# Three engines' share of a layer norm moved to one: GpSimd takes all but VectorE's statistics

## The chip, the cores and the metric

The kernel runs on one core of a Trainium2 chip, as one launch. The metric is the device time of that launch in microseconds. Engines are called by the profile's names: PE is TensorE (PEld its weight loads), DVE is VectorE, ACT is ScalarE, POOL is GpSimd, SP is SyncE. They run side by side, each through its own list of instructions in a fixed order, and wait for each other on semaphores.

## The reference

The input is x, 8 sequences of 256 tokens with 128 features, all float32. Four blocks follow each other, each of the form x + f(layernorm(x)):

- a state-space block (Mamba style) with 16 states: its own RMS norm, a projection, a 4-tap convolution, softplus steps, a scan over time per state, a gate, an output projection;
- a mixture of 8 experts with 352 inner features, top 2 of 8 (called FFN here);
- an attention block with squared ReLU scores;
- the same mixture of experts again.

What matters here is the norm in front of each block:

```python
def _layernorm(x, axis=-1, eps=1e-05):
    m = jnp.mean(x, axis=axis, keepdims=True)
    v = jnp.var(x, axis=axis, keepdims=True)
    return (x - m) / jnp.sqrt(v + eps)
```

In front of the state-space block an RMS norm with its own epsilon follows. Both are folded into one factor per token: (variance times (1 + 1e-6) + 1e-11) to the power -1/2.

So there are 4 norms for each of 8 sequences: 8 called `m_*` (state-space) and 24 called `n_*` (16 in front of an FFN, 8 in front of attention).

## The kernel before

Tokens lie on the 128 partitions, so that a sequence is two halves (c = 0 and 1) of 128 tokens by 128 features: `X[:, u, c, :]`. A norm makes two tiles 128x128 (`m_xn` or `n_xn`), PE transposes them into a PSUM bank, ACT rounds them to a high part (`xhi`), DVE takes the remainder (`xlo`), and from then on PE multiplies with three products per weight tile (lines 1028 to 1030).

Who does what in a norm before the change:

- DVE, `m_stats`/`n_stats`: `bn_stats` for each half (line 798), `bn_aggr` for each half (line 801), then variance plus epsilon on a 128x2 tile (`m_ve` line 811, `n_ve` line 916).
- POOL, `m_pow`/`n_pow`: that tile to the power -1/2 (lines 407 and 414), giving `m_r`/`n_r`.
- DVE, `m_nb`/`n_nb`: minus mean times that factor (lines 816 and 921), giving `m_b`/`n_b`.
- ACT, `m_norm`/`n_norm`: factor times x plus that bias, one instruction for each half (lines 533 and 652), with one signal behind the second.
- PE, `m_turn`/`n_turn`: two transposes (line 1023) behind that one signal.

The order of all the work is set by one plan. `build_plan` gives every step of every sequence a due time from hand-set tables (`AT`, `NORM`, `M_IN`, `SHIFT`, ...), sorts the steps by it, and each engine issues its own steps in that order (`run_schedule`). The state-space scan of sequence u overlaps the FFNs and attention of the sequences before it, one period of some 70 us for each sequence; behind the last scan only FFN and attention work is left.

POOL's steps in the scan of one sequence are, for each of 16 states, a product with C (`mulC`, line 455, waits for DVE's scan of that state, line 891) and a running sum (`sum`, line 468), about 1.3 us each; then the convolution (lines 426 and 437), `m_delta` (line 447) and `m_gate` (line 475). The due time of `n_norm` lies 1.5 us behind that of `n_pow`. In the sorted plan a step of POOL's scan work falls between the two for almost every `n` norm of a sequence whose scan is still running, for example:

```
n_pow(q3), sum(3,0), n_norm(q3), m_norm(4), mulC(3,1)
n_pow(q8), mulC(5,9), n_norm(q8), sum(5,9)
```

Here q counts the 16 FFNs in their order, so that q0 is the first FFN of sequence 0, and odd q (up to 13) are first FFNs, even q from 2 on second FFNs; a0 to a7 are the attention norms; (3,1) is state 1 of sequence 3. For q0 a `mulC(1,0)` stands between `n_pow` and `n_norm`, and for the attention norm a3 the first product of a convolution (`m_mul1(6)`). Behind the last scan nothing stands between them.

Of the kernel before, what the change touches and what calls it, by code (L numbers as in the profile page):

```python
# [5 lines left out]
ALU = mybir.AluOpType  # L6
# [47 lines left out]
 m_var m_rstd m_nb m_xm m_xt m_hi m_lo m_ph m_pad m_tap0 m_tap m_sum m_conv0 m_h m_xp m_xe m_dt m_abs m_e m_u m_ln m_v m_pos m_delta m_dx m_y0  # L54
 m_pg m_g m_dA m_dbx m_scan m_p m_ysum m_yacc m_yg m_out m_x1
 n_var n_rstd n_nb n_xm n_xt n_hi n_lo r_lg r_dd r_th r_w2 r_w
# [11 lines left out]
M_IN = {"m_stats": -0.78, "m_pow": -1.32, "m_nb": -0.06, "m_norm": 1.88, "m_turn": 2.37, "m_hi": 3.09, "m_lo": 2.98,  # L68
# [5 lines left out]
NORM = {"n_stats": -0.39, "n_pow": 1.17, "n_nb": 1.18, "n_norm": 2.67, "n_turn": 3.85, "n_hi": 4.96, "n_lo": 4.64}  # L74
# [14 lines left out]
SHIFT = {"m_stats": [0.5, -67.8, -1.1], "m_pow": [-15.2, -60.3, -0.2], "m_nb": [0.2, -65.6, 0],  # L89
         "m_norm": [-11.5, -58.6, 0.2], "m_turn": [0.1, -59.4, 2.5], "m_hi": [0.3, -54.7, 0.5],  # L90
# [95 lines left out]
def build(nc, x, vecs, in_w, xproj_w, dt_w, out_w, gate_w, up_w, down_w, uv_w, wo_w, row_b, router_w, out):  # L186
    schedule = build_plan()
    norms = norm_order(schedule)
    with ExitStack() as ctx:
# [46 lines left out]
        m_b = sb("m_b", [P, NC])  # L236
# [23 lines left out]
        n_b = sb("n_b", [P, NC])  # L260
# [131 lines left out]
        def _(pool):  # L392
# [84 lines left out]
            run_schedule({"setup": setup, "m_pow": m_pow, "n_pow": n_pow, "m_mul1": conv_product(1), "m_add1": conv_sum(1),  # L477
# [4 lines left out]
        def _(act):  # L482
# [43 lines left out]

            def m_norm(u):

                act.wait_ge(s["m_nb"], u + 1)
                if u:  # L530
                    act.wait_ge(s["m_xt"], u)
                for c in range(NC):
                    ins = nc.scalar.activation(m_xn[:, c, :], X[:, u, c, :], ACT.Identity, bias=m_b[:, c:c + 1],
                                               scale=m_r[:, c:c + 1])
                ins.then_inc(s["m_xm"], 1)
# [108 lines left out]
            def n_norm(arg):  # L644
                l = norms[arg]
                kind, k = arg
# [663 lines left out]
```

## Time and profile before

| what | value |
|---|---|
| median of 3 runs | 674.01 us (668.97 to 675.3) |
| profiled execution, its own time | 673.67 us |
| its span, first to last instruction | 672.1 us |
| PE busy | 583.7 us (87%) |
| DVE busy | 527.1 us (78%) |
| POOL busy | 400.0 us (60%) |
| ACT busy | 395.5 us (59%) |
| mean granted TensorE clock | 0.937 |

The profiled execution's time is its span and 1.57 us around it, and lies 0.34 us under the median. Busy shares are means over stages with different limits: up to about 62 us the first scan runs with little else, from 62 to 566 us scans, FFNs and attention overlap, and from 566 us on POOL has only the norms' powers to do.

### The profile page before, as it was taken

Reading aid. Unit: us, or ns where it says so; the run is one execution under the profiler, and the core shown is the slowest. Engines: PE = TensorE matmul, PEld = TensorE weight load, DVE = VectorE, ACT = ScalarE, POOL = GpSimd, SP = SyncE. Lnnn points to the kernel's source line nnn. Section 1 sums busy time; section 2 is a strip of 40 time slices with the busy share of each in tenths; the row PEclk is TensorE's granted clock in tenths of the full one; section 3 lists DMA queues with packets and bytes.
Section 4 is the critical chain, followed back from the end, with each engine's and each line's share of the span. In section 5 each row is a group of like instructions: output and inputs, shape, how many; then the busy total and the mean of one; then the engine's idle time right before and its main releaser. Section 6 shows DMA issues by size and latency. Waiting matters only on the chain.

```text
span 672.1 us, 12742 instructions
## 1 busy us (share of the span) xinstructions
PE 583.7 (87%) x4370; PEld 550.3 (82%) x4370; DVE 527.1 (78%) x1162; ACT 395.5 (59%) x804; POOL 400.0 (60%) x338
## 2 busy tenths in 40 slices
PE   2566891399896999999999989999999999999998
PEld 1222791299896998989998989899989999999998
DVE  5789898667788789997899879988998897545454
ACT  6877566256567584777567674967585741515230
POOL 1296699858566586849775976778775665000000
PEclk9978896579798798989999998999997999999999
DMA  8725013111111110121122112031204000000000
GB/s 297 266 74 189 13 67 125 63 32 54 59 72 63 72 60 31 63 82 65 68 73 77 71 65 76 11 136 66 75 2 145 1 13 1 22 1 13 1 21 9
DMA packets 18162, 45.30 MB, mean 67 GB/s; under 512 B 2799, under 2 KB 13488, under 8 KB 13746
## 3 DMA queue, kind: packets, MB, share of 16 engines
q1 hardware_dynamic: 18098, 44.49, 18.9%
q8 instruction: 35, 0.57, 0.4%
q14 instruction: 29, 0.24, 0.1%
HBM read 40.02 MB, written 1.31 MB: 61 GB/s over the span
## 4 chain that ended last, share of the span: by engine, by line
PE 65%; DVE 11%; POOL 7%; issue 5%; ACT 3%; DVEq 0%; ACTq 0%; POOLq 0%
PE ps L1179 15%; PE ps L1028 14%; PE ps L1030 14%; PE ps L1029 14%; POOL yacc L468 3%; POOL st L455 2%; DVE X L992 2%; PE ps L1228 2%; DVE st L891 2%; DVE ps L877 1%; PE ps L1096 1%; PE ps L1241 1%; PE ps L1219 1%; DVE n_bn L798 1%; ACT L489 1%
## 5 line engine op out<-in xcount | busy, mean ns | idle before, releaser
L455 POOL TENSOR_TENSOR st<-st,rows_ring 128x512 f32<-128x512 f32 x128 | 168.1, 1314 | 98.1 <-DVE st L891 97.9
L1179 PE MATMUL ps<-down,inner_ring 128*128 128x128 f32 (+1 forms) x1408 | 172.2, 275 | 0.0
L1179 PEld LDWEIGHTS ps<-down,inner_ring 128*128 128x128 f32 (+1 forms) x1408 | 166.3, 192 | 1.1 <-DVE X L992 0.2
L686 ACT ACTIVATE sg<-ps 128x512 f32<-128x512 f32 x176 | 104.9, 597 | 100.9 <-PE ps L1030 99.0
L891 DVE TENSOR_TENSOR_SCAN st<-dA,ps 128x512 f32<-128x512 f32 x128 | 155.4, 1214 | 5.6 <-PE ps L1129 2.5
L978 DVE TENSOR_TENSOR inner_ring<-sg,ps 128x512 f32<-128x512 f32 x176 | 119.1, 679 | 47.5 <-ACT sg L686 24.7
L468 POOL TENSOR_TENSOR yacc<-yacc,st 128x512 f32<-128x512 f32 x112 | 144.5, 1290 | 7.1
L1028 PE MATMUL ps<-xhi,gate_hi 128*128 128x256 f32 x352 | 105.8, 301 | 19.0 <-DVE xlo L928 19.0
L641 ACT ACTIVATE dA<-delta,A 128x255 f32<-128x255 f32 x256 | 105.8, 494 | 8.5 <-POOL delta L447 7.4
L1028 PE MATMUL ps<-xhi,up_hi 128*128 128x256 f32 x352 | 106.3, 302 | 0.4 <-DVE inner_ring L978 0.3
L1029 PE MATMUL ps<-xlo,up_hi 128*128 128x256 f32 x352 | 102.9, 292 | 0.0
L1030 PE MATMUL ps<-xhi,up_lo 128*128 128x256 f32 x352 | 102.8, 292 | 0.0
L1029 PE MATMUL ps<-xlo,gate_hi 128*128 128x256 f32 x352 | 102.6, 291 | 0.0
L1030 PE MATMUL ps<-xhi,gate_lo 128*128 128x256 f32 x352 | 102.5, 291 | 0.0
L877 DVE TENSOR_TENSOR ps<-ps,rows_ring 128x512 f32<-128x512 f32 x128 | 88.4, 691 | 1.2
L1028 PEld LDWEIGHTS ps<-xhi,gate_hi 128*128 128x128 f32 x352 | 70.5, 200 | 22.6 <-issue 14.1
L992 DVE SCALAR_TENSOR_TENSOR X<-ps,wts,X 128x128 f32<-128x128 f32 x256 | 76.0, 342 | 13.7 <-PE ps L1179 13.7
L1028 PEld LDWEIGHTS ps<-xhi,up_hi 128*128 128x128 f32 x352 | 70.8, 201 | 1.4 <-DVE inner_ring L978 1.2
L1029 PEld LDWEIGHTS ps<-xlo,up_hi 128*128 128x128 f32 x352 | 71.0, 202 | 0.1
L1030 PEld LDWEIGHTS ps<-xhi,up_lo 128*128 128x128 f32 x352 | 70.8, 201 | 0.0
L1029 PEld LDWEIGHTS ps<-xlo,gate_hi 128*128 128x128 f32 x352 | 70.6, 201 | 0.1
L1030 PEld LDWEIGHTS ps<-xhi,gate_lo 128*128 128x128 f32 x352 | 70.5, 200 | 0.0
(145 smaller groups left out, 812.3 us busy)
## 6 DMA issues: line engine op xcount, KB each, us to landing
rows_ring<-bc SPq DMA_DIRECT2D x32, 1024.0 KB, 4.8
moved_rows<-inner_ring SPq DMA_DIRECT2D x96, 32.0 KB, 1.8
inner_ring<-gate_w SPq DMA_DIRECT2D x1, 1408.0 KB, 8.3
inner_ring<-up_w SPq DMA_DIRECT2D x1, 1408.0 KB, 10.8
down<-down_w SPq DMA_DIRECT2D x2, 512.0 KB, 10.8
out<-X SPq DMA_DIRECT2D x8, 128.0 KB, 1.8
X<-x SPq DMA_DIRECT2D x1, 896.0 KB, 5.4
down<-down_w SPq DMA_DIRECT2D x1, 384.0 KB, 8.4
```

The costliest lines, as they stand in the source:

```text
L455: nc.gpsimd.tensor_tensor(st[:, i % NST], st[:, i % NST], row, ALU.mult).then_inc(s["m_p"], 1)
L468: nc.gpsimd.tensor_tensor(yacc[:, u % 2], yacc[:, u % 2], st[:, i % NST], ALU.add).then_inc(s["m_yacc"], 1)
L641: ins = nc.scalar.activation(dA[:, i % NDA, it, 1:], delta[:, it, 1:], ACT.Exp, scale=A[:, it, n:n + 1])
L686: nc.scalar.activation(sg[:, k % 2], two(bank_of(q, 2 * j)), ACT.Silu).then_inc(s["f_sg"], 1)
L877: nc.vector.tensor_tensor(states_in(u, n), dxps, row, ALU.mult).then_inc(s["m_dbx"], 1)
L891: nc.vector.tensor_tensor_scan(out=st[:, i % NST].rearrange(flat), data0=dA[:, i % NDA].rearrange(flat), data1=states_in(u, n).rearrange(f ...
L978: nc.vector.tensor_tensor(inner[:, j], sg[:, k % 2], two(bank_of(q, 2 * j + 1)), ALU.mult).then_inc(s["f_in"], 1)
L992: nc.vector.scalar_tensor_tensor(out=X[:, u, c, :], in0=part, scalar=wts[:, q % 2, c, e:e + 1], in1=X[:, u, c, :], op0=ALU.mult, op1=ALU.a ...
L1028: nc.tensor.matmul(bank, w[0], xv[0], start=start, stop=False)
L1029: nc.tensor.matmul(bank, w[0], xv[1], start=False, stop=False)
L1030: return nc.tensor.matmul(bank, w[1], xv[0], start=False, stop=stop)
L1179: ins = nc.tensor.matmul(bank_of(q, 2 * NP + e)[:, c * H:(c + 1) * H], act_in, down[0:rows, e, n, :], start=n == 0, stop=n == NB - 1)
```

## The change

DVE keeps the statistics and signals each `bn_aggr`. POOL does the rest: variance plus epsilon, power, and (x - mean) times factor for each half, each half with its own signal. PE waits for the signal of a half in front of the transpose of that half. The DVE steps `m_nb` and `n_nb` are gone, and the steps `m_norm` and `n_norm` keep their due times but are now in POOL's list and not in ACT's. DVE's `n_stats` (and `m_stats` from the second on) newly waits until POOL has done the norm before it, since POOL now reads the mean from `n_mv`.

```diff
@@ POOL
             def m_pow(u):
-                pool.wait_ge(s["m_var"], u + 1)
+                pool.wait_ge(s["m_var"], NC * (u + 1))
+                nc.gpsimd.tensor_scalar(m_ve[:], m_mv[:, :, 1], 1.0 + RMS_EPS, RMS_EPS * EPS, ALU.mult,
+                                        ALU.add).then_inc(s["m_eps"], 1)
+                pool.wait_ge(s["m_eps"], u + 1)
                 nc.gpsimd.tensor_tensor(m_r[:], m_ve[:], neghalf[:], ALU.pow).then_inc(s["m_rstd"], 1)
 
+            def m_norm(u):
+                pool.wait_ge(s["m_rstd"], u + 1)
+                if u:
+                    pool.wait_ge(s["m_xt"], u)
+                for c in range(NC):
+                    nc.gpsimd.tensor_scalar(m_xn[:, c, :], X[:, u, c, :], m_mv[:, c, 0:1], m_r[:, c:c + 1], ALU.subtract,
+                                            ALU.mult).then_inc(s["m_xm"], 1)
+
             def n_pow(arg):
+                pool.wait_ge(s["n_var"], NC * (norms[arg] + 1))
+                nc.gpsimd.tensor_scalar(n_ve[:], n_mv[:, :, 1], EPS, None, ALU.add).then_inc(s["n_eps"], 1)
+                pool.wait_ge(s["n_eps"], norms[arg] + 1)
+                nc.gpsimd.tensor_tensor(n_r[:], n_ve[:], neghalf[:], ALU.pow).then_inc(s["n_rstd"], 1)
+
+            def n_norm(arg):
                 l = norms[arg]
-                pool.wait_ge(s["n_var"], l + 1)
+                kind, k = arg
+                u = k if kind == "a" else QUEUE[k][0]
+                pool.wait_ge(s["n_rstd"], l + 1)
                 if l:
-                    pool.wait_ge(s["n_xm"], l)
-                nc.gpsimd.tensor_tensor(n_r[:], n_ve[:], neghalf[:], ALU.pow).then_inc(s["n_rstd"], 1)
+                    pool.wait_ge(s["n_xt"], l)
+                for c in range(NC):
+                    nc.gpsimd.tensor_scalar(n_xn[:, c, :], X[:, u, c, :], n_mv[:, c, 0:1], n_r[:, c:c + 1], ALU.subtract,
+                                            ALU.mult).then_inc(s["n_xm"], 1)
@@ ACT (m_norm of the same form goes too)
-            def n_norm(arg):
...
-                for c in range(NC):
-                    ins = nc.scalar.activation(n_xn[:, c, :], X[:, u, c, :], ACT.Identity, bias=n_b[:, c:c + 1],
-                                               scale=n_r[:, c:c + 1])
-                ins.then_inc(s["n_xm"], 1)
@@ DVE, n_stats (m_stats in the same way)
-                norm_stats(u, n_bn, n_mv)
-                nc.vector.tensor_scalar(n_ve[:], n_mv[:, :, 1], EPS, None, ALU.add).then_inc(s["n_var"], 1)
-
-            def n_nb(arg):
                 l = norms[arg]
-                dve.wait_ge(s["n_rstd"], l + 1)
-                nc.vector.scalar_tensor_tensor(out=n_b[:], in0=n_mv[:, :, 0], scalar=-1.0, in1=n_r[:], op0=ALU.mult,
-                                               op1=ALU.mult).then_inc(s["n_nb"], 1)
+                if l:
+                    dve.wait_ge(s["n_xm"], NC * l)
+                for c in range(NC):
+                    mark(nc.vector.bn_stats(n_bn[:, c, :], X[:, u, c, :]))
+                link()
+                for c in range(NC):
+                    nc.vector.bn_aggr(n_mv[:, c, :], n_bn[:, c, :]).then_inc(s["n_var"], 1)
@@ PE, n_turn (m_turn in the same way)
-                pe.wait_ge(s["n_xm"], l + 1)
-                transposes(chainps, n_xn[:].rearrange("p c h -> p (c h)")).then_inc(s["n_xt"], 1)
+                for c in range(NC):
+                    pe.wait_ge(s["n_xm"], NC * l + c + 1)
+                    ins = nc.tensor.transpose(chainps[:, c * P:(c + 1) * P], n_xn[:, c, :], ident[:])
+                ins.then_inc(s["n_xt"], 1)
```

The tables lose their entries for `m_nb` and `n_nb`; no other due time changes.

## Rows read from the trace of the kernel before

**Rows 1.** The page: span, TensorE's busy time, engines of the chain that ended last.

```profile
span 672.1 us, 12742 instructions
...
PE 583.7 (87%) x4370; PEld 550.3 (82%) x4370; DVE 527.1 (78%) x1162; ACT 395.5 (59%) x804; POOL 400.0 (60%) x338
...
PE 65%; DVE 11%; POOL 7%; issue 5%; ACT 3%; DVEq 0%; ACTq 0%; POOLq 0%
```

**Rows 2.** PE's waits: who for whom, us in total, times, longest.

```profile
PE ps L1092 <- POOL yacc L475: 23.4, 1, 23.4
PE ps L1028 <- DVE xlo L928: 19.0, 15, 2.3
...
PE ps L1023 <- ACT m_xn L533: 9.2, 6, 5.9
```

**Rows 3.** Two stretches: us, each engine's busy time, PEclk, DMA share, GB/s.

```profile
62.00:128.00 66.00, 37.62 (x275) 34.72 (x275) 55.05 (x99) 33.66 (x75) 55.30 (x45) 0.81 0.24 84
...
566.00:672.00 106.00, 99.90 (x833) 98.36 (x831) 52.02 (x162) 34.13 (x73) 3.45 (x5) 1.00 0.04 11
```

**Rows 4.** Groups of the norms: busy us, mean ns; idle before, by releaser.

```profile
L652 ACT ACTIVATE n_xn<-X,n_b,n_r 128x128 f32<-128x128 f32 x48 | 20.9, 484 | 49.7 <-DVE n_b L921 49.6
L414 POOL TENSOR_TENSOR n_r<-n_ve,neghalf 128x2 f32<-128x2 f32 x24 | 16.6, 693 | 87.9 <-DVE n_ve L916 87.0
...
L921 DVE SCALAR_TENSOR_TENSOR n_b<-n_mv,n_r 128x2 f32<-128x2 f32 x24 | 9.3, 386 | 1.5 <-POOL n_r L414 1.4
...
L533 ACT ACTIVATE m_xn<-X,m_b,m_r 128x128 f32<-128x128 f32 x16 | 7.0, 482 | 10.2 <-DVE m_b L816 10.2
...
L916 DVE TENSOR_SCALAR n_ve<-n_mv 128x2 f32<-128x2 f32 x24 | 5.5, 228 | 0.8
...
L816 DVE SCALAR_TENSOR_TENSOR m_b<-m_mv,m_r 128x2 f32<-128x2 f32 x8 | 3.3, 418 | 5.1 <-POOL m_r L407 5.1
...
L811 DVE TENSOR_SCALAR m_ve<-m_mv 128x2 f32<-128x2 f32 x8 | 2.2, 279 | 0.3
```

**Rows 5.** Groups of other POOL instructions, by shape.

```profile
L426 POOL TENSOR_TENSOR tap<-xpad,vec 128x512 f32<-128x512 f32 x21 | 21.9, 1042 | 22.9 <-ACT xpad L554 22.8
...
L396 POOL TENSOR_SCALAR_AFFINE_SELECT ident<-ident 128x128 f32<-128x128 f32 x1 | 0.3, 292 | 0.2 <-POOL ident L394 0.2
...
L402 POOL TENSOR_SCALAR_AFFINE_SELECT one_at<-one_at 128x1 f32<-128x1 f32 x1 | 0.2, 185 | 0.1
```

**Rows 6.** Timeline at q5: start us, us, instruction, idle before it.

```profile
286.90 1.27 POOL L468 TENSOR_TENSOR yacc<-yacc,st 128x512 f32<-128x512 f32 x1
287.27 0.92 DVE L921 SCALAR_TENSOR_TENSOR n_b<-n_mv,n_r 128x2 f32<-128x2 f32 x1
...
290.97 0.41 PE L1023 MATMUL ps<-ident,m_xn 128*128 128x128 f32 x2 [0.36 <-ACT m_xn L533]
```

**Rows 7.** Timeline at q0.

```profile
70.47 1.91 POOL L455 TENSOR_TENSOR st<-st,rows_ring 128x512 f32<-128x512 f32 x1 [0.46 <-DVE st L891]
...
71.41 0.44 PE L1023 MATMUL ps<-ident,n_xn 128*128 128x128 f32 x2 [0.43 <-ACT n_xn L652]
```

**Rows 8.** Timeline at q1 and a0.

```profile
132.21 1.27 POOL L455 TENSOR_TENSOR st<-st,rows_ring 128x512 f32<-128x512 f32 x1 [0.47 <-DVE st L891]
...
132.87 0.47 DVE L798 BATCH_NORM_STATS2 n_bn<-X 128x6 f32<-128x128 f32 x2
...
135.71 0.55 PE L1028 MATMUL ps<-xhi,gate_hi 128*128 128x256 f32 x1 [1.60 <-DVE xlo L928]
```

**Rows 9.** Timeline at q8, the second FFN of a sequence.

```profile
398.58 1.71 POOL L455 TENSOR_TENSOR st<-st,rows_ring 128x512 f32<-128x512 f32 x1 [0.96 <-DVE st L891]
...
399.61 0.41 PE L1023 MATMUL ps<-ident,n_xn 128*128 128x128 f32 x2
```

**Rows 10.** Timeline at q15, the last norm.

```profile
640.10 0.39 PE L1023 MATMUL ps<-ident,n_xn 128*128 128x128 f32 x2
...
641.49 0.36 PE L1028 MATMUL ps<-xhi,gate_hi 128*128 128x256 f32 x1 [1.01 <-DVE xlo L928]
```

More of the change, by code:

```diff
@@ L66 @@
 PERIOD = 70.0
-M_IN = {"m_stats": -0.78, "m_pow": -1.32, "m_nb": -0.06, "m_norm": 1.88, "m_turn": 2.37, "m_hi": 3.09, "m_lo": 2.98,
+M_IN = {"m_stats": -0.78, "m_pow": -1.32, "m_norm": 1.88, "m_turn": 2.37, "m_hi": 3.09, "m_lo": 2.98,
         "m_ph": 4.27, "m_pad": 5.67, "m_tap0": 6.74, "m_mul1": 5.59, "m_add1": 6.17, "m_mul2": 7.27, "m_add2": 7.49,
@@ L73 @@
 M_OUT = {"m_gate": 3.81, "m_out": 3.98, "m_res": 6.18}
-NORM = {"n_stats": -0.39, "n_pow": 1.17, "n_nb": 1.18, "n_norm": 2.67, "n_turn": 3.85, "n_hi": 4.96, "n_lo": 4.64}
+NORM = {"n_stats": -0.39, "n_pow": 1.17, "n_norm": 2.67, "n_turn": 3.85, "n_hi": 4.96, "n_lo": 4.64}
 ROUTE = {"r_logits": -0.6, "r_top": 0.9, "r_index": 0.93, "r_th": 1.68, "r_w2": 2.1, "r_spread": 1.56,
@@ L475, in m_gate @@
                 nc.gpsimd.tensor_tensor(yacc[:, u % 2], yacc[:, u % 2], gact[:], ALU.mult).then_inc(s["m_yg"], 1)
-            run_schedule({"setup": setup, "m_pow": m_pow, "n_pow": n_pow, "m_mul1": conv_product(1), "m_add1": conv_sum(1),
+            run_schedule({"setup": setup, "m_pow": m_pow, "m_norm": m_norm, "n_pow": n_pow, "n_norm": n_norm, "m_mul1": conv_product(1), "m_add1": conv_sum(1),
                           "m_mul2": conv_product(2), "m_add2": conv_sum(2), "m_mul3": conv_product(3), "m_add3": conv_sum(3), "m_delta": m_delta, "mulC": mulC,
@@ L642, in decay @@
                 ins.then_inc(s["m_dA"], 1)
-            def n_norm(arg):
-                l = norms[arg]
-                kind, k = arg
-                u = k if kind == "a" else QUEUE[k][0]
-                act.wait_ge(s["n_nb"], l + 1)
-                if l:
-                    act.wait_ge(s["n_xt"], l)
-                for c in range(NC):
-                    ins = nc.scalar.activation(n_xn[:, c, :], X[:, u, c, :], ACT.Identity, bias=n_b[:, c:c + 1],
-                                               scale=n_r[:, c:c + 1])
-                ins.then_inc(s["n_xm"], 1)
             def n_hi(arg):
@@ L794, in split_uv @@
                 nc.vector.tensor_tensor(uv_lo[:], uv_raw, uv_hi[:].bitcast(F32), ALU.subtract).then_inc(s["w_vl"], 1)
-            def norm_stats(u, bn, mv):
-                for c in range(NC):
-                    mark(nc.vector.bn_stats(bn[:, c, :], X[:, u, c, :]))
-                link()
-                for c in range(NC):
-                    mark(nc.vector.bn_aggr(mv[:, c, :], bn[:, c, :]))
-                link()
             def m_stats(u):
@@ L1019, in free @@
                     pe.wait_ge(s[sem], value)
-            def transposes(bank, src):
-                for c in range(NC):
-                    ins = nc.tensor.transpose(bank[:, c * P:(c + 1) * P], src[:, c * P:(c + 1) * P], ident[:])
-                return ins
             def three(bank, w, xv, start=True, stop=True):
@@ L1038, in m_turn @@
                 free(bank_name(u))
-                pe.wait_ge(s["m_xm"], u + 1)
-                transposes(mamba(u), m_xn[:].rearrange("p c h -> p (c h)")).then_inc(s["m_xt"], 1)
+                for c in range(NC):
+                    pe.wait_ge(s["m_xm"], NC * u + c + 1)
+                    ins = nc.tensor.transpose(mamba(u)[:, c * P:(c + 1) * P], m_xn[:, c, :], ident[:])
+                ins.then_inc(s["m_xt"], 1)
                 reader[bank_name(u)] = ("m_lo", u + 1)
```

39 lines of the change are left out of this document (14 added, 25 removed).

## The prediction

> **What bounds the kernel now.** The page comes first: PE is busy 583.7 of 672.1 us, and the chain that ended last runs over PE for 65% and over DVE for 11% [rows 1]. So the question is what a norm makes PE wait for, and PE's own waits answer it [rows 2]. The longest, 23.4 us, is one event: PE waits at 127 us for the end of a scan that POOL sets. The stretches show POOL busy 55.3 of 66 us there, at a granted clock of 0.81 [rows 3]; this is the one stretch in which POOL's own work is on the path. Of the rest, 19.0 us in 15 places is the first FFN product waiting for `xlo`, and 9.2 us in 6 places is a transpose waiting for ACT's `m_xn`; 5.9 of these are the kernel's start.
>
> How much of the 19.0 belongs to the norm? At the last norm the transpose starts without an idle time in front of it: PE still had the FFN before to finish. What follows is transpose, rounding, remainder, product, with a wait of 1.01 us that this change does not touch [rows 10]. All four norms in front of an FFN behind the last scan look like this. So of the 19.0 us, 15 x 1.01 = 15.2 are a floor. In the tail from 566 us on PE is busy 99.9 of 106 us [rows 3], and nothing is to be had.
>
> **What it removes.** From ACT 20.9 + 7.0 = 27.9 us, from DVE 9.3 + 5.5 + 3.3 + 2.2 = 20.3 us [rows 4]. The mean of `n_b` is 386 ns for two elements a partition; rows 6 show why. It starts at 287.27 inside a POOL sum and ends at 288.19, with that sum (288.17): the DVE instruction is held until POOL is done. Six `n_b` in front of FFNs are held so, for about 0.9 to 1.2 us; one of them stands there.
>
> The Trainium skill (SBUF — State Buffer, "Who interferes with whom") says that a VectorE instruction with two SBUF inputs and a GpSimd instruction that reads SBUF exclude each other for the whole of whichever started first. By that rule, the trace agrees, the 64 new POOL instructions would hold two-input DVE work in turn.
>
> **What it adds to POOL,** for each norm: one instruction on 2 columns, and one on 128 columns for each half. The trace has neither. For the small one the nearest row is the 185 ns on one column; between that and the 693 ns of the power I take 0.2. For the half the ends are 0.29 (the one-input instruction of the same shape) and 1.04 (a product on four times the columns); a line between 185 ns at 1 column and 1042 at 512 gives 0.40 [rows 5, 4]. I take 0.4, near the lower end since that row has the very shape, and keep both. A step that waits for the one before it on POOL idled 0.2 us in the only row that names such a wait, in the kernel's start [rows 5]; between a product and the sum that needs it the timeline leaves some 0.08, and I take that. So a norm takes POOL 0.2 + 0.08 + 0.69 + 0.08 + 0.8 = 1.85 us behind the last `bn_aggr`, of which 1.15 are new, 37 us for 32. Before, with no queue, it was 0.2 + 0.08 + 0.69 + 0.19 + 0.88, about 2.05. The chain by itself is no longer than it was, and the second signal gives PE a half early that then waits for the other.
>
> The Trainium skill (GPSIMD Engine Reference, "Performance versus the Vector engine") speaks against elementwise work on GpSimd, about half of VectorE's rate, yet gives some 1.03 cycles an element for short one-input loops. An estimate from it, 0.11 us above a fixed 0.19, would make a half 0.3 us and the sum 2 us smaller. No run here shows it yet.
>
> POOL has room for 1.15 us: it idles 87.0 us in front of `n_r` [rows 4]. What counts is its order: the halves now queue behind a step of the scan.
>
> **Place by place, on PE's path:**
>
> - Start: the chain loses about 0.2 us, -0.2.
> - q0: `n_norm` stands behind `mulC(1,0)`, which ends at 72.38, so the halves end at 73.2; PE transposed at 71.41 [rows 7]. Behind that transpose stand, in PE's order, the projection whose result POOL's convolution waits for, and the gate product. +1.1, and it goes into the stretch that POOL then fills to 127 us.
> - The eps step of `m_pow(3)` falls in front of the gate at the end of that stretch: +0.3.
> - q1 and a0: `n_norm(q1)` comes behind `mulC(2,1)` (133.48), so ends near 134.5. DVE's `n_stats(a0)`, at 132.87 before, must newly wait for it, and `m_xlo` and `xlo` queue behind. A held `n_ve` of over 1 us there is gone. The gate product at 135.71 moves by about +0.7 [rows 8].
> - Second FFNs q2 to q12: `n_norm` waits for `mulC`. At q8 that ends at 400.29, the halves at 401.1, while PE transposed at 399.61 [rows 9]; as `xlo` was late for another reason (DVE was busy for over 1 us more), PE loses only about 0.45. The pattern repeats at q6, q10 and q12: 4 x 0.5 = +2.0. At q4 the halves end 0.6 us before the transpose: 0.
> - a3: the first convolution product stands in between, +0.7.
> - Gains: at the six places of a held `n_b` DVE comes free 0.9 to 1.2 us earlier. Five belong to odd q, and at three of these the wait of 0.36 us for `m_xn` goes too, as ACT is out of it [rows 6]; the new `m_norm` ends about 289.8, before 290.97. But `n_stats` of the next norm now has to wait for POOL's halves, and the 1.01 floor stays. I take -0.65 each, -3.9.
> - ACT's 27.9 us: in the tail ACT waits anyway, elsewhere its norms were beside PE's work. 0 beyond the above.
> - Tail: 0, covered by the FFN before; without that cover 0.2 us a norm would be gained.
>
> Sum: -0.2 + 1.1 + 0.3 + 0.7 + 2.0 + 0.7 - 3.9 = +0.7. From 673.67 that is 674.4, and against the median of 674.01 about the same: **674 us**. What a measurement of this kernel can tell from no change is about 1%, 6.7 us.
>
> **Rivals.**
>
> *A. A half on POOL is dear (slower).* The place is the pair of halves between scan steps. At 1.04 us a half each norm ends 1.3 later. That adds 1.3 at the start, q0, q1 and a3 (5.2), 6.1 over q2 to q12, about 7.7 at the odd q, where `n_norm` and `m_norm` follow each other (2.6 for the pair, less the slack to PE's transpose), 0.5 in the tail: 19.5, so 694. It passes 1% from about 0.6 us a half on (0.4 + 0.64 x 6/19.5). For it: two-element powers cost 0.69, so POOL's cost depends on the operation, and the per-partition operands are in none of its rows. Against: the 0.29 us row. Chance 0.15, at a typical 0.7 us 683.
>
> *B. The relief pays in full (faster).* DVE and ACT are what the overlapped stages queue for; if every wait in front of a first FFN product falls to the floor, 19.0 - 15.2 = 3.8 come back, with the transposes' waits outside the start 9.2 - 5.9 = 3.3 [rows 2], and some 1 us of knock-on: 666. For it: six held `n_b`. Against: the scan steps in POOL's order, rows 7 to 9. Chance 0.11.
>
> *C. The change does not do what it says.* It keeps the other due times, and PE needs both halves before its signal, so the signal per half alone gives at most a transpose, 0.2 us a norm, where PE waits. This ends as no change, in the middle case.
>
> **How the numbers follow.** Forecast case 0.74, rival A 0.15, rival B 0.11. The forecast's own range is 670 to 679: the ends of a half's cost near my value (0.29 gives -3.4, 0.55 gives +4.6). The 8-in-10 range reaches half way into the rivals: 667 to 683. Faster by over 1% (under 667.3): 0.12, slower by over 1% (over 680.7): 0.16, within: 0.72.
>
> **What would show it.** Right: a new POOL group on 128 columns near 0.4 us x64; PE waiting for POOL's `n_xn` at q0, q1 and the second FFNs, a few tenths to 1.5 us each; DVE's `bn_stats` of a0 waiting for POOL; no wait at the transposes of the tail; DVE busy near 507, ACT near 368, POOL near 437 us. Wrong: halves over 0.6 us; transposes in the tail that wait; a granted clock other than 0.81 in the stretch to 128 us or 1.00 in the tail, which would move PE's time with no wait to name.

## The result and the profile after

The change makes the kernel a little slower: 675.91 us as the median of 13 executions (673.91 to 680.47) against 674.01, now also of 13 (666.38 to 675.3), a ratio of 1.007 with an interval of 1.0035 to 1.0104. A second build of it gave 1.0077 [1.0041, 1.0113]. The profiled execution took 675.79 us.

The ratio is not that of the two medians, which is 1.0028. The kernel before took 666.4 to 670.1 us six times and 674.0 to 675.3 seven times, the changed one 673.9 to 676.5 eight times and 679.0 to 680.5 five times, so a median can jump by some 5 us with one execution, and a ratio over all of them is the safer number wherever two kernels are compared below. Of the two profiled executions the one before (673.67) lies at the upper group of its kernel, the one after (675.79) in the lower group of its own. Ratios leave out an execution that lies over 1.5% above the fastest of its kernel, which matters for one version below, where that is five of 11.

The page after, against [rows 1]:

```profile
span 674.2 us, 12717 instructions
...
PE 575.1 (85%) x4370; PEld 536.9 (80%) x4370; DVE 509.6 (76%) x1098; ACT 371.0 (55%) x740; POOL 461.0 (68%) x434
...
PE 39%; POOL 30%; issue 13%; DVE 7%; ACT 2%; POOLq 0%; DVEq 0%; ACTq 0%
```

DVE gave up 17.5 us, ACT 24.5, and POOL took on 61. The chain that ended last ran over POOL for 7% before and runs over it for 30% now. The groups of the norms, against [rows 4] (busy us, mean ns, then idle before):

```profile
L431 POOL TENSOR_SCALAR n_xn<-X,n_mv,n_r 128x128 f32<-128x128 f32 x48 | 38.4, 808 | 0.5
...
L421 POOL TENSOR_TENSOR n_r<-n_ve,neghalf 128x2 f32<-128x2 f32 x24 | 17.2, 717 | 2.0
L414 POOL TENSOR_SCALAR m_xn<-X,m_mv,m_r 128x128 f32<-128x128 f32 x16 | 14.2, 894 | 0.3
...
L419 POOL TENSOR_SCALAR n_ve<-n_mv 128x2 f32<-128x2 f32 x24 | 5.6, 234 | 71.1 <-DVE n_mv L907 70.8
L404 POOL TENSOR_SCALAR m_ve<-m_mv 128x2 f32<-128x2 f32 x8 | 4.1, 508 | 13.0 <-DVE m_mv L802 12.8
```

A half costs 0.81 us, not the 0.40 that I took, and the small operation 0.23. Of POOL's 61 us more the forecast had 37. TensorE's waits, against [rows 2] (us, times, longest):

```profile
PE ps L1074 <- POOL yacc L493: 24.1, 1, 24.1
PE ps L1008 <- DVE xlo L913: 13.3, 12, 1.7
PE ps L1021 <- POOL m_xn L414: 13.3, 14, 5.9
...
PE ps L1088 <- POOL n_xn L431: 10.2, 17, 2.7
```

The wait for `xlo` fell from 19.0 to 13.3, `m_xn` rose from 9.2 to 13.3, and the 10.2 us in 17 places for `n_xn` are new but for 0.8. In sum TensorE waits 7.8 us longer for the norms, and is busy 8.6 us less (583.7 to 575.1) for the same 4370 matmuls. Two stretches of the same trace, against [rows 3]:

```profile
62.00:128.00 66.00, 38.38 (x275) 34.18 (x275) 56.59 (x100) 36.05 (x79) 58.12 (x48) 0.85 0.19 68
...
566.00:674.00 108.00, 101.83 (x866) 99.88 (x865) 52.40 (x158) 30.11 (x63) 15.88 (x23) 1.00 0.04 10
```

The kernel's start, timeline after (start us, us, instruction, idle before it). VectorE and POOL hold each other:

```profile
15.90 1.59 DVE L773 TENSOR_TENSOR gate_lo<-inner_ring,gate_hi 128x1408 fp32r<-128x1408 f32 x1
16.07 1.47 POOL L404 TENSOR_SCALAR m_ve<-m_mv 128x2 f32<-128x2 f32 x1 [9.55 <-DVE m_mv L802]
17.62 0.71 POOL L407 TENSOR_TENSOR m_r<-m_ve,neghalf 128x2 f32<-128x2 f32 x1
18.11 1.63 DVE L773 TENSOR_TENSOR gate_lo<-inner_ring,gate_hi 128x1408 fp32r<-128x1408 f32 x1 [0.62 <-ACT gate_hi L528]
18.44 2.74 POOL L414 TENSOR_SCALAR m_xn<-X,m_mv,m_r 128x128 f32<-128x128 f32 x2
```

The small operation starts inside VectorE's split of the gate weights and ends (17.54) just behind it (17.49): 1.47 us for what takes 0.19 alone. The pair of halves takes 2.74 where it takes 1.58 elsewhere. So the second norm's transposes start at 20.46 instead of 18.39; 0.46 of these 2.07 us were there before, since the first norm's rounding comes at 7.09 instead of 6.62. In the second build's trace it is the power that is held there, 2.02 us long. The gate step that ends the first scan, before and after:

```profile
65.22 0.68 DVE L900 TENSOR_TENSOR yacc<-ps,gact 128x512 f32<-128x512 f32 x1
```

```profile
68.62 0.68 DVE L885 TENSOR_TENSOR yacc<-ps,gact 128x512 f32<-128x512 f32 x1
```

That is 3.4 us (2.6 in the second build, with 67.85). A second hold stands right in front of this step, POOL's `m_ve` at 65.77 (1.44 us) beside VectorE's split of the up weights; it costs nothing that can be seen here, since the version below that takes away only the first hold still has it and reaches this step at 65.20. Executions differ at the start in any case: the gate weights landed at 12.99 us in the trace before, at 13.52 in this one and at up to 14.25 in others. Then q0, q5, q8 and q15, against [rows 6, 7, 9, 10]:

```profile
72.84 0.72 POOL L421 TENSOR_TENSOR n_r<-n_ve,neghalf 128x2 f32<-128x2 f32 x1
...
73.61 1.83 POOL L473 TENSOR_TENSOR st<-st,rows_ring 128x512 f32<-128x512 f32 x1
...
75.44 1.57 POOL L431 TENSOR_SCALAR n_xn<-X,n_mv,n_r 128x128 f32<-128x128 f32 x2
...
77.07 0.48 PE L1088 MATMUL ps<-ident,n_xn 128*128 128x128 f32 x1 [0.45 <-POOL n_xn L431]
...
289.88 1.57 POOL L414 TENSOR_SCALAR m_xn<-X,m_mv,m_r 128x128 f32<-128x128 f32 x2
...
290.82 0.30 PE L1021 MATMUL ps<-ident,m_xn 128*128 128x128 f32 x1 [0.36 <-POOL m_xn L414]
...
398.65 1.63 POOL L473 TENSOR_TENSOR st<-st,rows_ring 128x512 f32<-128x512 f32 x1 [0.57 <-DVE st L876]
400.27 1.57 POOL L431 TENSOR_SCALAR n_xn<-X,n_mv,n_r 128x128 f32<-128x128 f32 x2
...
401.21 0.30 PE L1088 MATMUL ps<-ident,n_xn 128*128 128x128 f32 x1 [1.15 <-POOL n_xn L431]
...
403.24 0.36 PE L1008 MATMUL ps<-xhi,gate_hi 128*128 128x256 f32 x1 [1.01 <-DVE xlo L913]
...
640.74 1.58 POOL L431 TENSOR_SCALAR n_xn<-X,n_mv,n_r 128x128 f32<-128x128 f32 x2
...
644.45 0.36 PE L1008 MATMUL ps<-xhi,gate_hi 128*128 128x256 f32 x1 [1.01 <-DVE xlo L913]
```

Between the power and the first half stands a step of the scan. In this trace that is so at 19 of 24 norms (at a3 it is a convolution product, at q1 the two halves of an `m` norm stand there as well), the first such step at 73.61 and the last at 539.84 us; from the end of the power to the first half 30.8 us pass in sum at these 19. The five norms from 572 us on have none.

**Where the time went.** In these two traces the changed kernel is 7.35 us behind at q1's gate product (143.06 against 135.71), 1.4 at q8's (403.24 against 401.86) and 3.0 at q15's (644.45 against 641.49). So a large loss comes early and most of it is given back. From q1's gate product to q8's TensorE does the same work in both (length, busy time of PE, PEld, DVE, ACT, POOL, granted clock, DMA; before, after, and the second build):

```profile
135.71:401.86 266.15, 250.28 (x1915) 244.18 (x1916) 222.59 (x492) 176.53 (x358) 189.13 (x156) 0.94 0.18 64
```

```profile
143.06:403.24 260.18, 242.28 (x1916) 233.23 (x1916) 214.51 (x465) 165.15 (x330) 214.14 (x198) 0.97 0.19 65
```

```profile
144.14:408.00 263.86, 246.72 (x1915) 238.66 (x1916) 215.40 (x465) 165.17 (x330) 213.97 (x198) 0.95 0.18 64
```

The changed kernel's TensorE is busy 8.0 us less and idle 2.0 us more: what it gives back here is TensorE's clock. How much that is depends on the execution. The second build's profiled one took 679.64 us; it is 8.4 us behind at q1, 6.1 at q8 (408.00) and 6.7 at q15 (648.17), so it gave back far less. The product behind q8's wait for `xlo`, and the stretches around it in the kernel before:

```profile
401.86 0.36 PE L1028 MATMUL ps<-xhi,gate_hi 128*128 128x256 f32 x1 [1.84 <-DVE xlo L928]
```

```profile
397.00:403.00 6.00, 4.16 (x37) 3.93 (x36) 6.00 (x15) 3.20 (x6) 4.91 (x5) 1.00 0.18 74
403.00:407.00 4.00, 4.00 (x23) 4.00 (x23) 3.10 (x14) 1.57 (x6) 2.48 (x2) 0.57 0.03 8
```

The same in the relief version of the experiments:

```profile
395.32 0.36 PE L1031 MATMUL ps<-xhi,gate_hi 128*128 128x256 f32 x1 [1.19 <-DVE xlo L931]
```

```profile
395.00:399.00 4.00, 3.68 (x31) 3.71 (x32) 3.87 (x13) 2.23 (x6) 3.92 (x4) 1.00 0.00 0
```

Behind the wait of 1.84 us the granted clock falls to the 1.2 GHz level for 3.5 us: a product of 256 columns takes 0.41 us instead of 0.28, and the next follows after 0.213 instead of 0.118. Behind the wait of 1.19 it stays at 1.00. That is one pair of places and no rule: in the changed kernel the clock falls at q8 too (0.51 from 404.6 to 408.0 us), behind waits of 1.15, 0.39 and 1.01. From 80 us on the kernel before has eight stretches at the lower level and the changed one six. The first of them is 37.5 us long in both and covers the long wait at the end of the second scan; the others last 3 to 7 us each, 34 us in seven before and 27 in five after, and 34 in nine in the second build.

### The profile page after: what moved, and what is told of

Read it like the earlier page. It is cut to its first block, busy times and chain, and to the rows that moved or that the text cites. A ratio compares the mean times of both kernels' runs of the same rounds, so it can differ in the third digit from the quotient of the medians.

```text
span 674.2 us, 12717 instructions
## 1 busy us (share of the span) xinstructions
PE 575.1 (85%) x4370; PEld 536.9 (80%) x4370; DVE 509.6 (76%) x1098; ACT 371.0 (55%) x740; POOL 461.0 (68%) x434
## 4 chain that ended last, share of the span: by engine, by line
PE 39%; POOL 30%; issue 13%; DVE 7%; ACT 2%; POOLq 0%; DVEq 0%; ACTq 0%
POOL yacc L486 10%; POOL st L473 10%; PE ps L1163 9%; PE ps L1008 8%; PE ps L1009 8%; PE ps L1010 8%; POOL n_xn L431 3%; PE ps L1212 2%; PE ps L1078 1%; POOL conv L455 1%; POOL n_r L421 1%; POOL m_xn L414 1%; DVE n_bn L904 1%; DVE X L977 1%; PE ps L1225 1%
## 5 line engine op out<-in xcount | busy, mean ns | idle before, releaser
L1008 PE MATMUL ps<-xhi,gate_hi 128*128 128x256 f32 x352 | 103.4, 294 | 13.3 <-DVE xlo L913 13.3
L1008 PE MATMUL ps<-xhi,up_hi 128*128 128x256 f32 x352 | 104.4, 297 | 1.7 <-DVE inner_ring L963 1.5
L1009 PE MATMUL ps<-xlo,gate_hi 128*128 128x256 f32 x352 | 100.3, 285 | 0.0
L1010 PE MATMUL ps<-xhi,gate_lo 128*128 128x256 f32 x352 | 100.1, 284 | 0.0
L1009 PE MATMUL ps<-xlo,up_hi 128*128 128x256 f32 x352 | 99.9, 284 | 0.0
L1010 PE MATMUL ps<-xhi,up_lo 128*128 128x256 f32 x352 | 99.8, 283 | 0.0
L1008 PEld LDWEIGHTS ps<-xhi,up_hi 128*128 128x128 f32 x352 | 68.9, 196 | 3.7 <-DVE inner_ring L963 2.9
L1009 PEld LDWEIGHTS ps<-xlo,gate_hi 128*128 128x128 f32 x352 | 68.9, 196 | 0.1
L1009 PEld LDWEIGHTS ps<-xlo,up_hi 128*128 128x128 f32 x352 | 68.7, 195 | 0.1
L1010 PEld LDWEIGHTS ps<-xhi,up_lo 128*128 128x128 f32 x352 | 68.5, 195 | 0.0
```

Source lines behind the costliest of these rows:

```text
L1008: nc.tensor.matmul(bank, w[0], xv[0], start=start, stop=False)
L1009: nc.tensor.matmul(bank, w[0], xv[1], start=False, stop=False)
L1010: return nc.tensor.matmul(bank, w[1], xv[0], start=False, stop=stop)
```

## The experiments

Each run states its expectations as they were recorded; letters name theories within one group of runs only. "Ratio" is against the kernel before, run beside it. The edits are shown shortened.

**1. Which norms cost.** The change built again; only the 24 n norms on POOL; only the 8 m norms; and all but the m norms of sequences 0 and 1, which stay as before. (In these versions VectorE's `m_stats` still waits for the norm before it, also where that is not on POOL.)

```diff
+def on_pool(kind, k):          # a2: "n" only   a3: "m" only   a4: all but m(0), m(1)
+    return k in MP if kind == "m" else NP_ALL(kind, k)
```

> The changed kernel once more, unaltered, as the yardstick of this group. Theory L (the halves and the epsilon step on POOL are held by VectorE's two-input weight splits at the start, then queue between scan steps): 6 to 7 us slower than before where both have the same TensorE clock stretches. In the profile the first scan's gate step (DVE yacc) near 68.6 us against 65.2 before and the end of the second scan's gate (PE's output projection) near 132.4 against 127.3. Theory C (the loss is the TensorE clock and nothing else): gate step of the first scan as before within 0.5 us.

> Only the 24 norms in front of FFN and attention are done on POOL; the 8 state-space norms are done as before the change, by all three engines. Theory L: no POOL instruction meets the split of the gate weights near 16 us, so the first scan's gate step returns to 65.2 to 65.5 us; what is left is the q0, q1 and a0 queueing, +3 at 127 us; 3 us faster than the changed kernel. Rival Q (all of the loss is the queueing of the n halves between scan steps): no faster than the changed kernel.

> Only the 8 state-space norms are done on POOL, the 24 others as before the change. Theory L: the first scan's gate step at 68.4 to 68.8 us as in the changed kernel (+2.3 from the hold behind the split of the gate weights, +0.7 from that of the up weights, some 0.4 from the first norm), then no further loss to 127 us; 3 to 4 us slower than before. Rival Q: as fast as before within 1 us.

> As the changed kernel, but the state-space norms of the first two sequences, which fall into the start, are done as before. Theory L: first scan's gate step near 65.9 us (only the 0.7 from the up weights' split is left), 2.7 us faster than the changed kernel, and 3 to 4 us slower than before. Rival Q: as the changed kernel within 1 us.

Measured: 676.8 us, 1.0077 [1.0041, 1.0113]; n alone 677.45, 1.0106 [1.0051, 1.016]; m alone 672.82, 1.0032 [0.9989, 1.0075]; all but m(0), m(1) 684.03, 1.0186 [1.0125, 1.0248]. By the ratios the loss is with the n norms, though the intervals of the second and third overlap. The gate step of the first scan came at 66.16 us with n alone and at 66.85 with m alone, where 65.2 to 65.5 and 68.4 to 68.8 were expected. The last version is a miss that I can't explain: its gate step came at 66.1 us, 2.5 us earlier than in the changed kernel, as it should, and the whole was still slower by 8 us (7 by the ratios). In its trace, of 682.11 us, the waits for the norms are smaller than in the changed kernel's, 33.4 us against 36.8 (`xlo`, `m_xn`, `n_xn`); TensorE's busy time is larger, 584.3 against 575.1 for the same 4370 matmuls.

**2. The start, the place in POOL's order, the two VectorE steps.** Four kernels: the kernel before with some 2.2 us of extra VectorE work at its start; the change with the due time of `n_norm` right behind the power; the change with VectorE's splits of the gate weights made to wait for the first two m norms; and "relief": POOL takes epsilon, power and minus mean times factor (on 128x1), ACT keeps the two passes of 128x128.

```diff
 b1  m_stats(0), DVE:
+    for _ in range(4): memset(at_s)
 b2  NORM:
-    "n_norm": 2.67
+    "n_norm": 1.1701
 b3  split_gate, DVE:
+    dve.wait_ge(s["m_xm"], 2 * NC)
 b4  n_pow, POOL (kernel before otherwise; m_pow likewise):
+    n_ve = n_mv[:, :, 1] + EPS            # was DVE's
+    for c in range(NC): n_b[:, c] = n_mv[:, c, 0] * n_r[:, c] * -1.0   # was DVE's
```

Wherever POOL makes `n_b`, VectorE's next `n_stats` waits for it, as it waits for the halves in the change. The expectation of the third speaks of the gate and the up weights; the edit holds back only the gate weights' splits.

> The kernel before with nothing changed but a pure delay of some 2 us: VectorE clears an unused tile four times in front of the first norm's statistics. Theory S (what is lost at the start is carried to the end, and the rest is a matter of which idle gaps of PE are followed by a stretch at the lower TensorE clock): 2 us slower on average, 675 us, with single executions between 667 and 680 and slow-clock stretches behind 200 us at other norms than in the profile of before. Rival H (slack behind the start hides it): 673 us, as before.

> As the changed kernel, but the due time of the n norm's halves is put right behind that of the power, so that no scan step of POOL stands between them in front of FFN and attention. Theory Q (the halves queue behind a scan step): q0's transposes start near 74.9 us and not 76.3, q1's and the second FFNs' 1.3 us earlier relative to their statistics; the stretch from the first scan's gate to the second scan's residual falls from 66.0 to 64.5 us; 3 us faster than the changed kernel, near 673. Rival G (the halves' own 0.79 us is what counts, wherever they stand): within 1 us of the changed kernel.

> As the changed kernel, but VectorE's splits of the weights (gate and up) wait until POOL has done the second state-space norm, so that at 16 us the two cannot hold each other. Theory L: POOL's epsilon step and halves there take 0.2 and 1.6 us (1.4 and 2.7 with the split beside them), the second transpose of that norm ends near 19 us and not 21.5, and delta of the first scan comes near 26.0 to 26.5 us instead of 27.5 to 27.8; 1.5 us faster than the changed kernel. Rival D (a late weight transfer and not the held POOL sets delta): delta at 27.5 to 27.8 as in the changed kernel.

> Half of the change: POOL takes over variance plus epsilon, power, and minus mean times factor (on one column for each half), ACT keeps the two 128x128 instructions of each norm. VectorE is relieved as in the changed kernel, POOL gets no 128-column work. Theory P (the 0.79 us halves on POOL are the loss and the relief of VectorE is a gain): 1 to 3 us faster than before, 671, and 5 us faster than the changed kernel. Rival N (relief of VectorE is worth nothing, moving anything to POOL's queue costs): as before or up to 3 us slower.

Measured: delay 675.33, 1.0036 [1.0002, 1.007]; near place **668.0, 0.9924** [0.9896, 0.9953]; splits wait 674.69, 1.0023 [0.9991, 1.0055]; relief **662.71, 0.9836** [0.9797, 0.9876]. The near place alone turns the change from a loss into a gain, some 10 us by the ratios where 3 were expected: of the edits to the order, the signals and the norms that the change leaves on POOL, none does as much alone. TensorE's wait for `n_xn` and its timeline at q8:

```profile
PE ps L1088 <- POOL n_xn L431: 2.0, 3, 1.5
```

```profile
395.77 0.72 POOL L421 TENSOR_TENSOR n_r<-n_ve,neghalf 128x2 f32<-128x2 f32 x1
396.59 1.66 POOL L431 TENSOR_SCALAR n_xn<-X,n_mv,n_r 128x128 f32<-128x128 f32 x2
...
398.30 0.39 PE L1088 MATMUL ps<-ident,n_xn 128*128 128x128 f32 x2
```

The halves start 0.1 us behind the power, and PE's transposes start without idle time, where in the changed kernel they waited 1.15 us. The start with the splits made to wait:

```profile
16.00 0.19 POOL L404 TENSOR_SCALAR m_ve<-m_mv 128x2 f32<-128x2 f32 x1 [9.56 <-DVE m_mv L803]
...
17.09 1.57 POOL L414 TENSOR_SCALAR m_xn<-X,m_mv,m_r 128x128 f32<-128x128 f32 x2
```

0.19 and 1.57 us instead of 1.47 and 2.74: that they were long before came from the overlap with the splits. The gate step is back at 65.2 us. The whole gains 0.5% on the change (1.0023 against 1.007 and 1.0077, with intervals that overlap). Relief is 11 us faster than the kernel before, where its theory P had 1 to 3. What relief removes from the wait for `xlo`, and what its two new POOL operations cost:

```profile
PE ps L1031 <- DVE xlo L931: 13.5, 15, 1.2
```

```profile
L428 POOL TENSOR_SCALAR n_b<-n_mv,n_r 128x1 f32<-128x1 f32 x48 | 13.2, 291 | 2.4
```

**3. The length of a half, the signal, and relief by parts.** The change with each n half done twice in its place; the change with TensorE waiting for both halves before the first transpose; relief with the splits waiting; relief for the n norms alone.

```diff
 c1  n_norm, POOL, in front of each half:
+    nc.gpsimd.tensor_scalar(n_xn[:, c, :], X[:, u, c, :], ...)   # the same half
+    ...                                                          # and wait for it
 c2  n_turn, PE (m_turn likewise):
-    pe.wait_ge(s["n_xm"], NC * l + c + 1)
+    pe.wait_ge(s["n_xm"], NC * (l + 1))
 c3  relief, split_gate, DVE:
+    dve.wait_ge(s["m_nb"], 2 * NC)
 c4  relief, m norms as in the kernel before
```

> The change as made, but each of the 48 POOL halves of the n norms is computed twice (the second overwrites the first with the same values). This doubles the suspected cost alone. Theory H (the halves of the n norms stand on TensorE's path at their 0.8 us): a norm's second half lands 1.6 us later, so in the places where TensorE waits for n_xn (17 waits in the changed kernel) the wait grows by 1.6 us, in the others POOL uses its slack; between 684 and 698, ratio 1.015 to 1.035 against the kernel before. Theory S (the start alone made the difference, the n halves lie beside other work): as the changed kernel, 674 to 679.

> The change as made, but TensorE waits for both halves before the first transpose, as in the kernel before, so that only the signal for each half is undone. The first transpose then starts 0.8 us later, the second, which is the one that ends the group, where it did. Theory H and my rival C agree: as the changed kernel within 1 us, 675 to 678. If the overlap of half and transpose pays, 24 norms by about 0.3 us at most, up to 683.

> The version with POOL's epsilon, power and minus mean times factor on 128x1 and ScalarE's two 128x128 passes, and in it VectorE's start splits of the gate weights wait for the first two norms' small POOL work. Theory K (VectorE's two-input splits and POOL hold each other at the start): POOL's first steps of the second norm no longer stand behind the splits (1.47 us for an operation of 0.2), the second norm's transposes come at or before 18.8 us instead of about 20, the first gate step up to 2 us earlier, whole kernel 660 to 662.7. Rival: the start is set by the arrival of the gate weights and no difference shows, 662 to 664.

> As the version with POOL's small operations and ScalarE's two passes, but for the 24 n norms alone; the 8 m norms are as in the kernel before. If the small POOL operations of the m norms cost at the start (they meet VectorE's splits), this is 1 to 2 us faster than with all norms, 660 to 662; if the m norms gain as the n norms do (VectorE's m_b off its queue), 1 to 2 us slower, 664 to 666. The n norms alone should keep at least 8 us of the gain against the kernel before.

Measured: twice **729.87, 1.0834** [1.078, 1.0888]; one signal 1.0087 [1.0044, 1.013]; relief with waiting splits 661.41, 0.982 [0.9775, 0.9865]; relief of n norms alone **659.91, 0.9813** [0.9755, 0.9872]. (The median of all 11 executions of the second is 682.19, 1.012 of the kernel before beside it; its ratio goes by six of them.)

Doubling cost 54 us (51 by the ratios), far beyond what I expected (at most 22), and more than the 38.2 us that the second halves take on POOL. The page and TensorE's waits of that kernel:

```profile
PE 606.7 (83%) x4370; PEld 568.7 (78%) x4370; DVE 513.9 (70%) x1098; ACT 371.5 (51%) x740; POOL 499.5 (68%) x482
```

```profile
PE ps L1091 <- POOL n_xn L434: 37.6, 29, 3.6
```

The wait for `n_xn` grew by 27.4 us, and TensorE's busy time by 31.6 for the same 4370 matmuls: those took longer. The mean granted clock fell from 0.927 to 0.890. So a late half is paid twice, as the wait and in the clock behind it. One signal or two makes no difference that this can tell (1.0087 against 1.007 and 1.0077), as my rival C had it; with all its executions counted, the one signal would look some 0.5% worse.

The relief of the n norms alone is the fastest kernel of the study, 14 us under the kernel before. Keeping the m norms as they were is worth 0.2% or nothing here; making the splits wait about as much.

**4. Place against length, once more.** Only the n norms on POOL, near place; the change in the near place with halves done twice; near place and splits waiting together; and the kernel before with only minus mean times factor moved to POOL (epsilon stays on DVE).

```diff
 d1  a2 with "n_norm": 1.1701        d2  c1 with "n_norm": 1.1701
 d3  b3 with "n_norm": 1.1701        d4  c4, n_ve on DVE as before
```

> Only the 24 n norms are on POOL, the 8 m norms are as in the kernel before, and the n halves stand right behind the power in POOL's order instead of behind the scan steps that come due first. Theory Q (the place in the queue is the price): 8 to 10 us faster than the n norms alone in their later place (1.0106), so 663 to 669, ratio 0.985 to 0.995. Theory L (the length of 0.79 us is the price): at most 2 us faster, 672 to 677.

> The change as made with the n halves right behind the power, and each half of the n norms computed twice. Against the single halves in the same place (0.9924): if the length counts once in full, two halves later by 1.6 us in the 17 norms that TensorE waits for, 24 to 30 us more, 692 to 700; if most of the halves' time is covered once nothing stands before them, up to 10 us more, 670 to 680. In the later place doubling cost 54 us.

> The change as made, the n halves right behind the power, and VectorE's start splits of the gate weights wait until POOL has done the first two norms. If the two causes are separate and add up: the first gate step at 65.2 instead of 67 us, and 665 to 667 for the whole. If what is won at the start is lost to another order later: 667 to 670.

> The kernel before, but minus mean times factor of the n norms is done on POOL (two operations of 128x1, 0.29 us each) right behind the power, where VectorE did it. Epsilon stays on VectorE, the 128x128 passes on ScalarE. Theory R (VectorE's n_b behind its scan queue was what delayed the norms, and takes VectorE's time twice): the gain of the version with both small operations on POOL, 659 to 664. Theory E (it is the epsilon and its two signals): 668 to 673.

Measured: **663.47, 0.9851** [0.9807, 0.9894]; twice in the near place 703.33, 1.0466 [1.0414, 1.0517]; both mends 665.88, 0.9889 [0.9844, 0.9934]; minus mean times factor alone 666.02, 0.9896 [0.9849, 0.9942]. For the n norms alone the place is worth 14 us by the medians and 17 by the ratios (1.0106 to 0.9851), more than the 8 to 10 I expected. With the near place the m norms on POOL cost something that can be seen: 0.9924 against 0.9851, and TensorE waits 15.5 us in 14 places for `m_xn`, against 7.8 in two where they stay as before. The length counts too: doubling in the near place costs 35.3 us, above my 24 to 30, 0.92 us for each us of POOL's. Theory L, that length was the price and place not, falls; but place is the price only because POOL's steps there are long. The mends of start and place add up, roughly (0.9924 to 0.9889, with intervals that overlap). One small VectorE step a norm, taken off its queue, gives over half of the relief of the n norms: 8.0 of 14.3 us. At 666.02 us that lies between the ranges of both theories, 659 to 664 and 668 to 673, so the epsilon step counts as well.

**5. Does the wait bring the clock down?** TensorE does 8 throwaway matmuls in front of the first gate product of q1 to q15, where it waits for `xlo`; in the kernel before and in the changed one.

```diff
 gate(q, 0), PE, q > 0, before the wait for n_lo:
+    for _ in range(8):
+        nc.tensor.matmul(bank, gate_hi[:, 0:P], gate_hi[:, 0:T], start=True, stop=True)
```

> The kernel before, but TensorE does 8 throwaway matmuls of 256 columns (gate weights against gate weights, into the bank that the product clears next; 0.94 us at 0.118 each) in front of the first gate product of q1 to q15, where it waits for xlo 0.9 to 2.3 us. Nothing else changes. Theory K (a wait of TensorE brings the stretch at the lower granted clock behind it): the stretches behind q2 to q12 go or get fewer, the clock's mean rises from 0.937 to 0.95 or more, TensorE's busy time falls in spite of 14 us of extra matmuls, and the kernel is 5 to 12 us faster, 662 to 669. Rival F (the clock has nothing to do with these waits): the matmuls lie in waits or cost up to 0.3 us each, 674 to 679.

> The change as made, with the same 8 throwaway matmuls in front of the first gate product of q1 to q15. Its waits for n_xn, in front of the transposes, stay unfilled. Theory K: the change loses less to the lower clock than the kernel before (six stretches against eight), so it gains less, 2 to 8 us, 668 to 674, and is then 1 per cent or more slower than the filled kernel before. Rival F: 676 to 681.

Measured: the kernel before with filled waits **663.58, 0.9841** [0.9795, 0.9887]; the changed one 668.05, 0.9929 [0.9895, 0.9963]. Rival F falls. In slices of a fortieth of the span the granted clock was, for the kernel before, and then filled:

```profile
PEclk9978896579798798989999998999997999999999
```

```profile
PE 588.0 (88%) x4490; PEld 554.2 (83%) x4490; DVE 528.0 (79%) x1162; ACT 394.7 (59%) x804; POOL 400.7 (60%) x338
...
PEclk9989798559997999999999999999999999999999
```

```profile
PE ps L1028 <- DVE xlo L928: 4.7, 7, 1.3
```

Behind the 13th slice the kernel before has five dips, the filled one none. The waits that were filled are 0.30 to 2.31 us long in the trace before. TensorE's busy time did not fall in spite of the extra matmuls, as theory K had it, but rose to 588.0. The 120 of them, 0.118 us apart, take 14 us; without them TensorE would be busy 574 us, 10 less than the 583.7 of [rows 1] for the same work. The median fell by 9.4 us, the profiled execution by 7.6 (673.67 to 666.09). With the wait for `xlo` replaced by matmuls of about the same length, what is left for the gain is the clock. The two filled kernels differ by 0.9% (0.9929 over 0.9841), as the two unfilled do, so the change doesn't lose by the clock at these waits. The new wait in front of them was not filled (10.3 us in 15 places for `n_xn` in the filled change's trace) and is the likely place; no run fills it.

## Why the prediction was wrong

I forecast no change, 674.0 from a sum of +0.7. It is 0.7% slower, with an interval that leaves out zero, inside my range of 667 to 683 and under the 1% bound that I had set. That it came so near is luck: the step that failed is the price of a half on POOL, some 12 us too low by my own rates, and the gains were put 7 to 10 us too low as well, with the opposite sign.

- **The half: failed.** "I take 0.4, near the lower end since that row has the very shape, and keep both." It took 0.81, twice as much, 0.78 at the least. The row of 0.29 us was a one-input instruction of 128x128, but another operation, and one with immediate operands; these halves read two values a partition. Which of the two makes the difference no run tells apart. The estimate from the Trainium skill (GPSIMD Engine Reference, "Performance versus the Vector engine") of 0.3 us was further off still: the trace disagrees with it for this form. By rival A's own rate, 19.5 us for 0.64, my costs of 4.8 (1.1 + 0.3 + 0.7 + 2.0 + 0.7) would have been 17.3 (4.8 + 19.5 x 0.41 / 0.64). What the halves cost can be measured: relief against the change is the two passes on ACT or on POOL, 0.9836 against 1.007, 2.3% or some 16 us, 13.2 by the medians. That holds the late place with the length, since relief has no halves in POOL's order at all. Also, my sentence that 0.3 us a half would make the sum 2 us smaller does not agree with my own rate, which gives 3.
- **The gains: failed the other way.** I took -3.9 and an end of -8 for rival B. In the changed kernel the five odd q gave none of it: TensorE's waits for `m_xn`, `n_xn` and `xlo` at q3 to q11 are 6.7 us in sum before and 6.9 after, since the wait for `m_xn` did not go with ACT but came back as one for POOL. It is the kernels without the halves on POOL that show what the relief is worth. Relief alone brought 11.3 us, and with the m norms left alone 14.3. My floor of 15 x 1.01 us was none: of the 15 waits for `xlo` before, three were shorter already (0.94, 0.56 and 0.30), and relief brought them from 19.0 to 13.5. The rows had shown me the held `n_b`; what I left out is the clock behind the wait. In relief's trace TensorE is busy 8.7 us less for the same matmuls (575.0 for 583.7). I had read the mean clock of two stretches [rows 3] as given, not as a thing that the waits of the norms set. Filling these waits is worth 9.4 us, about the size of the missing part.
- **The start: not in the sum.** "Start: the chain loses about 0.2 us, -0.2." It became 3.4 us longer up to the first gate step (2.6 in the second build), and the chain of the very first norm was not shorter but some 0.5 us longer. I cited the rule of the Trainium skill (SBUF — State Buffer, "Who interferes with whom") that a two-input VectorE instruction and GpSimd's reads exclude each other, and drew only one direction from it. The trace agrees with the other direction as well: VectorE's split of 1.6 us held POOL's 0.19 us step for 1.47. With the splits made to wait the first gate step is back at 65.2 us, and the whole gains 0.5%, with intervals that overlap.
- **q0, q1 and a0: right in kind, small.** The halves stand behind the scan step as said; at q0 they end at 77.0 instead of 73.2. Of the 5.7 us by which the last transpose is late, 3.4 are the start's; 2.3 stand against my 1.1, for which I gave no working; my own rows make it 73.2 - 71.41 = 1.8. At q1's gate product 1.7 more are lost (7.35 in all), for which I had 0.3 + 0.7; there the two halves of `m_norm(2)` stand in front of q1's in POOL's order as well, 2.8 us in all behind the power, and I had named only the scan step. DVE's `bn_stats` of a0 does wait for POOL, 3.6 us in the longest of its four waits.
- **Second FFNs: right within tenths where I had a loss.** TensorE's waits around q6, q8, q10 and q12 grew by 2.5 us in sum, for my 2.0. At q2 and q4 the wait for `xlo` fell by 1.2 and 0.6, where I had nothing. At q8 the scan step ends at 400.28, as I had it; the halves at 401.84 instead of 401.1. TensorE's waits around it go from 1.84 to 1.15 + 0.39 + 1.01, +0.7 for +0.5.
- **Tail: right.** No transpose waits at q15, the floor of 1.01 stays, cover as described [rows 10]. The granted clock is 1.00 there; in the stretch to 128 us it is 0.85 where I had named 0.81 as a sign. It is the same 37.5 us at the lower level in both traces, begun at 111.1 us instead of 106.4, and the stretch cuts it off.
- **Rival A** was the right mechanism at the right place, at 0.8 us a half; its 683 at 0.7 was too much only because rival B's relief was also true, and larger than priced. I gave them 0.15 and 0.11 as if only one could hold. **Rival C** holds for the signal per half.

What stays open: why the version without m(0) and m(1) on POOL is 8 us slower than the change (in its trace TensorE waits less and is busy longer), and what the m norms are worth at all, since leaving them as before is 0.7% faster beside near halves (0.9851 against 0.9924), 0.2% beside relief, and nothing or less beside late halves (1.0106 against 1.007). The delay of some 2.2 us at the start cost 0.36%, 2.4 us, so what is lost there is carried to the end; that a mere change of order can move this kernel by 1% isn't shown by it.

## What to carry to other kernels

Before a step is moved to an engine, look at what stands in front of it in that engine's order at the due time it keeps: here the scan step between power and halves cost some 10 us of the change and 17 of its n norms by the ratios (8 to 9 and 14 by the medians), by a due time kept from the time when another engine did it. Where TensorE waits in front of dense work, look at the granted clock of the next few us, and count a removed or added wait with what it does there. And price an elementwise pass by a row with the same operation and the same kind of operands, not only the same shape; of a chain of tiny steps move those to the idle engine that wait in a busy queue, and leave the wide pass where it is fast.

## What the runs showed of the hardware

- POOL's `tensor_scalar` on 128x128 with two operands that are one value a partition takes 0.78 us at the least and 0.81 in the mean; with one such operand and an immediate on 128x1 it takes 0.29; with immediates on 128x2 0.23, and 0.19 for one at the start. ACT does the 128x128 pass in 0.48 [rows 4].
- A step of POOL of 0.19 us took 1.47 when VectorE's two-input instruction on 1408 columns was under way (1.59 us), and a pair of halves 2.74 instead of 1.58.
- TensorE's granted clock fell to the 1.2 GHz level for 3 to 7 us at a time in the middle of the overlapped stages, as behind the wait of 1.84 us at q8. Throwaway matmuls in the waits for `xlo` kept it at 1.00 from 216 us on and made the kernel before 1.6% faster, with 14 us more work.
- Executions of one kernel differ by up to 9 us (666.38 to 675.3 before), and the places where the clock fell differ between two profiled executions of the changed kernel (five stretches from 150 us on, and nine).
